# A mixture-of-experts layer in 10 slots of four 32-place parts instead of 12 slots of two 64-place halves, with the next attention's keys split five and three

## What is computed

```python
def _L0_ffn_ref(hidden_states, router_w, gate_w, up_w, down_w):
    H, I, E = (256, 512, 8)
    x = hidden_states.reshape(-1, hidden_shape[-1])
    route = jax.nn.sigmoid(x @ router_w)
    max_ind = jnp.argmax(route, axis=1)
    max_prob = jnp.take_along_axis(route, max_ind[:, None], axis=1)
    for e in range(num_experts):
        mask = (max_ind == e)[:, None]
        h = jax.nn.silu(x @ gate_w[e]) * (x @ up_w[e])
        out = out + jnp.where(mask, h @ down_w[e], 0.0)
    out = out * max_prob

x = x + tanh(g_xattn[0]) * _L0_xattn_ref(_layernorm(x), ctx, ...)
x = x + tanh(g_ffn[0])   * _L0_ffn_ref(_layernorm(x), ...)
x = x + tanh(g_xattn[1]) * _L1_xattn_ref(_layernorm(x), ctx, ...)   # k = rms_norm(linear(ctx, k_w, k_b)), v = linear(ctx, v_w, v_b)
x = x + tanh(g_ffn[1])   * _L1_ffn_ref(_layernorm(x), ...)
```

## Time and profile before

| | us |
|---|---|
| median of 3 runs (740.77 to 741.91) | 741.28 |
| the profiled execution | 739.69 |
| its span, first to last instruction | 738.0 |
| PE busy in it, share | 715.3, 97% |
| ACT, DVE, POOL busy, share | 347.1 (47%), 429.1 (58%), 268.6 (36%) |
| keys and slot 0, from its first matmul to slot 1's | 100.56 to 111.09 |
| slots 1 and 2 | 111.09 to 121.21 |
| slots 3 to 10 | 121.21 to 170.14 |
| slot 11 and the last down part | 170.14 to 180.09 |

### The profile page before, as it was taken

How to read it: one execution, slowest core, us unless ns; L and a number is a source line. 1 busy time by engine, 2 the same in 40 slices (tenths; PEclk the granted TensorE clock), 3 DMA queues, 4 the chain that set the end, 5 groups by cost and what they waited for, 6 DMA issues and landing times.

```text
span 738.0 us, 13906 instructions
## 1 busy us (share of the span) xinstructions
PE 715.3 (97%) x4748; PEld 575.9 (78%) x4749; DVE 429.1 (58%) x796; ACT 347.1 (47%) x815; POOL 268.6 (36%) x387
## 2 busy tenths in 40 slices
PE   7999899999899999999999999999999999999997
PEld 6888654444677888899888999888788888888886
DVE  6888574222898755444554445545566665666565
ACT  4888323442677736455454454544532323232333
POOL 3232351111877656312213222121433444344330
PEclk9999999999999999999999999999999999999999
DMA  8980121111200001111010110100034343333421
GB/s 281 419 351 1 30 72 38 47 45 60 78 16 1 24 1 36 28 53 37 21 36 21 57 36 21 64 1 22 22 77 127 99 121 114 113 100 120 126 80 58
DMA packets 23497, 56.36 MB, mean 76 GB/s; under 512 B 3472, under 2 KB 12048, under 8 KB 22432
## 3 DMA queue, kind: packets, MB, share of 16 engines
q1 hardware_dynamic: 22688, 53.72, 22.1%
q0 software_dynamic: 768, 2.10, 0.9%
HBM read 50.49 MB, written 5.31 MB: 76 GB/s over the span
## 4 chain that ended last, share of the span: by engine, by line
PE 84%; ACT 5%; DVE 5%; POOL 3%; DMA 1%; issue 1%; SPq 0%; DVEq 0%; POOLq 0%; ACTq 0%
PE PS L352 17%; PE PS L354 17%; PE PS L353 16%; PE PS L1850 7%; PE PS L1516 6%; PE PS L1537 3%; PE PS L470 3%; PE PS L476 2%; PE PS L516 2%; PE PS L507 2%; PE PS L1856 2%; PE PS L529 2%; POOL Z L854 1%; ACT x_probT L683 1%; PE PS L458 1%
## 5 line engine op out<-in xcount | busy, mean ns | idle before, releaser
L1296 ACT ACTIVATE hhh<-hh 128x512 fp32r<-128x512 f32 x50 | 31.6, 632 | 103.7 <-DVE hh L1318 94.7
L352 PE MATMUL PS<-tTh,wh 128*128 128x512 f32 x200 | 78.3, 392 | 0.8 <-DVE tTl L673 0.5
L353 PE MATMUL PS<-tTl,wh 128*128 128x512 f32 x200 | 77.8, 389 | 0.0
L354 PE MATMUL PS<-tTh,wl 128*128 128x512 f32 x200 | 77.8, 389 | 0.0
L673 DVE TENSOR_TENSOR hhl<-hh,hhh 128x512 fp32r<-128x512 f32 x50 | 52.4, 1047 | 35.4 <-ACT hhh L1296 35.4
L1959 ACT ACTIVATE sm<-sm,nmx 128x128 f32<-128x128 f32 x128 | 49.7, 389 | 37.7 <-DVE nmx L2022 37.7
L1384 POOL CAST wh<-wraw 128x512 fp32r<-128x512 f32 (+1 forms) x50 | 26.1, 523 | 108.6 <-PE PS L354 108.6
L2061 POOL CAST ah<-araw 128x512 fp32r<-128x512 f32 (+1 forms) x32 | 16.2, 506 | 134.4 <-PE PS L354 134.4
L673 DVE TENSOR_TENSOR oTl<-PS,oTh 128x512 fp32r<-128x512 f32 x32 | 22.1, 691 | 71.6 <-ACT oTh L1953 71.6
L1386 POOL TENSOR_TENSOR wl<-wraw,wh 128x512 fp32r<-128x512 f32 (+1 forms) x50 | 58.0, 1161 | 8.4 <-POOL wh L1384 7.9
L352 PE MATMUL PS<-tTh,ah 128*128 128x512 f32 x128 | 53.1, 415 | 0.3 <-POOL al L2063 0.2
(11 more groups left out here) (279 smaller groups left out, 1903.2 us busy)
## 6 DMA issues: line engine op xcount, KB each, us to landing
WE<-moe SPq DMA_DIRECT2D x8, 1536.0 KB, 17.8
wraw<-moe SPq DMA_DIRECT2D x25, 384.0 KB, 3.1
araw<-attn SPq DMA_DIRECT2D x16, 384.0 KB, 3.1
cwb<-cw_d SPq DMA_DIRECT2D x20, 256.0 KB, 3.9
WX<-wx SPq DMA_DIRECT2D x4, 512.0 KB, 6.8
avraw<-attn_v SPq DMA_DIRECT2D x8, 256.0 KB, 3.2
cwb<-cw_d SPq DMA_DIRECT2D x4, 448.0 KB, 3.5
xs_d<-zeros SPq DMA_DIRECT2D x1, 1536.0 KB, 20.5
```

The source lines that it names most:

```text
L352: nc.tensor.matmul(out, wh_, xh_, start=first, stop=False, **kw)
L353: nc.tensor.matmul(out, wh_, xl_, start=False, stop=False, **kw)
L354: return nc.tensor.matmul(out, wl_, xh_, start=False, stop=last, **kw)
L1296: nc.scalar.activation(hhh[half][:, :], hh[half][:, :], ACT.Copy).then_inc(s.hi_done, 1)
```

## The change

`HALVES` of 64 places become `TILES` of 32: 1024 / 32 + 8 = 40 parts, four to a slot (`PARTS`), and 10 slots. The loop over slots turns twice instead of three times. Each round of matmuls of a slot now has four strips of 32 columns: part 0 reads `WE` at the register's address, parts 1 to 3 read fixed places, `part_weights`. Gate's stand in `WX[0]` (the first attention's weights, no longer used) and `w2`, up's in `w2`, down's in `w2` and in `FX` (the scattered rows, rows 0 to 3), and for the last slot in the gate's places. `y_s` moves into rows 4 and 5 of `FX`.

So nine copies of 128x1024 are made for a slot where there were three. ACT makes up's three, triggered by the end of up (`u_done`) instead of standing behind the x columns. DVE makes two of gate's, triggered by the end of gate (`g_done`), ahead of hs. POOL makes gate's third at `g_done`, and down's three for slot j when down of j-1 is done (before: one for j+1 when down of j was done). Slot 0 and the last slot have lists of their own. PE waits for all copies of a part ahead of its first matmul.

Of the keys, five batches instead of six are made ahead of and in slot 0 (`SOON` = 5), three behind the last. The filling matmuls ahead of the last transposes of keys go from 14 to 8, and ACT's masked keys of batch 1 move behind `queries(1)` in the attention's loop.

```diff
-HP = P // 2
-HALVES = T // HP + E0
-SLOTS = HALVES // 2
+PARTS = 4
+HP = P // PARTS
+TILES = T // HP + E0
+SLOTS = TILES // PARTS
+GU = C * I0
...
+SOON = 5
...
-        below = sb("below", [P, HALVES, E0], where=e)
+        below = sb("below", [P, TILES, E0], where=e)
...
-        exf = sb("exf", [P, HALVES], where=e)
-        ex = sb("ex", [P, HALVES], mybir.dt.int32, e)
+        exf = sb("exf", [P, TILES], where=e)
+        ex = sb("ex", [P, TILES], mybir.dt.int32, e)
...
-        w2 = sb("w2", [P, EW], where=e)
+        w2 = sb("w2", [P, 6 * GU], where=e)
+        part_weights = [[WX[0][:, q, :, :].rearrange("p c n -> p (c n)") for q in range(2)] + [w2[:, 0:GU]],
+                        [w2[:, k * GU:(k + 1) * GU] for k in (1, 4, 5)],
+                        [w2[:, k * GU:(k + 1) * GU] for k in (2, 3)] + [FX[:, 0:I0 // P, :].rearrange("p k n -> p (k n)")]]
...
-        y_s = [sb(f"y_s{i}", [P, D], where=e) for i in range(2)]
+        y_s = [FX[:, I0 // P + i, :] for i in range(2)]
...
-                for b in range(2):
+                def masked_keys(b):
...
+                masked_keys(0)
...
-                key_columns(act, MOST, B)
+                key_columns(act, SOON, B)
             def value_rows_back(n):
...
+                if n == -1:
+                    masked_keys(1)
...
-        def half_expert(eng, j, h):
-            return eng.value_load(ex[0:1, bass.ds(2 * j + h, 1)], min_val=0, max_val=E0 - 1)
+        def part_expert(eng, j, q):
+            return eng.value_load(ex[0:1, bass.ds(PARTS * j + q, 1)], min_val=0, max_val=E0 - 1)
...
+        def down_weights(j):
...
+            return part_weights[0 if is_last(j) else 2]
...
+        def part_copy(eng, e, mat, q, done, j=0):
+            dst, src = (down_weights(j) if mat == 2 else part_weights[mat])[q - 1], expert_part(e, mat * GU, GU)
+            if eng is nc.scalar:
+                m = eng.activation(dst, src, ACT.Copy)
+            else:
+                m = eng.tensor_copy(dst, src)
+            m.then_inc(done, 1)
...
         def expert_part(e, a0, n):
...
             def up(e, j, par, mat, done):
...
+                if mat == 0:
+                    pe.wait_ge(s.gate_copied, 2 * j + 2)
+                    pe.wait_ge(s.gate3_copied, j + 1)
+                else:
+                    pe.wait_ge(s.up_copied, 3 * j + 3)
...
-                    a0 = (mat * C + c) * I0
-                    out, x = PS[:, 2 * mat + par, :], xsT[par][:, c, :]
-                    nc.tensor.matmul(out[0:HP, :], x[:, 0:HP], expert_part(e, a0, I0), start=(c == 0), stop=(c == C - 1))
-                    pe.wait_ge((s.gate_copied, s.up_copied)[mat], 2 * j + c + 1)
-                    m = nc.tensor.matmul(out[HP:P, :], x[:, HP:P], w2[:, a0:a0 + I0], start=(c == 0), stop=(c == C - 1))
+                    for q in range(PARTS):
+                        w = expert_part(e, (mat * C + c) * I0, I0) if q == 0 else part_weights[mat][q - 1][:, c * I0:(c + 1) * I0]
+                        m = nc.tensor.matmul(PS[q * HP:(q + 1) * HP, 2 * mat + par, :], xsT[par][:, c, q * HP:(q + 1) * HP], w, start=(c == 0), stop=(c == C - 1))
...
             def turn_hidden(j):
...
             def down(j, par, between=None):
-                e = half_expert(pe, j, 0)
+                e = part_expert(pe, j, 0)
...
-                    a0 = 2 * C * I0 + k * D
-                    out = PS[:, 6 + par, 0:D]
-                    nc.tensor.matmul(out[0:HP, :], src[:, k, 0:HP], expert_part(e, a0, D), start=(k == 0), stop=(k == I0 // P - 1))
...
-                        pe.wait_ge(s.down_copied, j + 1)
-                    m = nc.tensor.matmul(out[HP:P, :], src[:, k, HP:P], w2[:, a0:a0 + D], start=(k == 0), stop=(k == I0 // P - 1))
+                        pe.wait_ge(s.down_copied, 3 * j + 3)
+                    for q in range(PARTS):
+                        w = expert_part(e, 2 * GU + k * D, D) if q == 0 else down_weights(j)[q - 1][:, k * D:(k + 1) * D]
+                        m = nc.tensor.matmul(PS[q * HP:(q + 1) * HP, 6 + par, 0:D], src[:, k, q * HP:(q + 1) * HP], w, start=(k == 0), stop=(k == I0 // P - 1))
...
             def tile(j, par, i):
-                e = half_expert(pe, j, 0)
+                e = part_expert(pe, j, 0)
...
-                    keys_values(5)
...
-                    pe.wait_ge(s.kv_free, 2 * MOST)
+                    pe.wait_ge(s.kv_free, 2 * SOON)
...
-            for i in range(MOST, B):
+            for i in range(SOON, B):
+                if i == B - 1:
...
+                    pe.wait_ge(s.y_ready, SLOTS - 1)
...
-                if i == MOST:
+                if i == SOON:
...
-                    fill(14, 2)
-                pe.wait_ge(s.k1_ready, 1 if i < MOST else 2)
+                    fill(8, 2)
+                pe.wait_ge(s.k1_ready, 1 if i < SOON else 2)
...
             def tile(j, par, i):
-                e = None if is_last(j) else half_expert(act, j + 1, 1)
+                es = [] if is_last(j) else [part_expert(act, j + 1, q) for q in range(1, PARTS)]
...
-                    gate_copies(e)
...
-                    return
-                if not is_second(j):
-                    hidden_columns(j - 1)
+                else:
+                    if not is_second(j):
+                        hidden_columns(j - 1)
+                    if not is_last(j):
+                        columns(j + 1, 1 - par)
...
-                    columns(j + 1, 1 - par)
-                    gate_copies(e)
...
-            def gate_copies(e):
-                for c in range(C):
-                    nc.scalar.activation(w2[:, c * I0:(c + 1) * I0], expert_part(e, c * I0, I0), ACT.Copy).then_inc(s.gate_copied, 1)
+                    act.wait_ge(s.u_done, j + 1)
+                    for q, e in enumerate(es):
+                        part_copy(nc.scalar, e, 1, q + 1, s.up_copied)
...
-            gate_copies(half_expert(act, 0, 1))
+            es = [part_expert(act, 0, q) for q in (3, 2)]
+            part_copy(nc.scalar, es[0], 0, 3, s.gate3_copied)
...
+            part_copy(nc.scalar, es[0], 1, 3, s.up_copied)
+            part_copy(nc.scalar, es[1], 1, 2, s.up_copied)
...
-            key_columns(act, 0, MOST)
+            key_columns(act, 0, SOON)
...
         def kv_bank(i):
...
-            return PS[:, (1, 7, 3)[i % 3] if i < MOST else 4 + i - MOST, :]
+            return PS[:, (1, 7, 3)[i % 3] if i < SOON else 4 + i - SOON, :]
...
         def normalise_keys(dve, i0, i1, group):
...
-            def up_copies(e):
-                for a0 in (C * I0, (C + 1) * I0):
-                    v.tensor_copy(w2[:, a0:a0 + I0], expert_part(e, a0, I0)).then_inc(s.up_copied, 1)
...
             def tile(j, par, i):
-                e = None if is_last(j) else half_expert(dve, j + 1, 1)
+                if not is_last(j):
+                    es = [part_expert(dve, j + 1, q) for q in (1, 2)]
+                    dve.wait_ge(s.g_done, j + 1)
+                    for q, e in enumerate(es):
+                        part_copy(v, e, 0, q + 1, s.gate_copied)
+                else:
+                    dve.wait_ge(s.g_done, j + 1)
...
+                    dve.wait_ge(s.down_copied, 3 * j)
+                    part_copy(v, part_expert(dve, j, 1), 2, 1, s.down_copied, j)
...
-                if not is_last(j):
-                    up_copies(e)
...
-                    keys_values(4, MOST)
+                    part_copy(v, part_expert(dve, 0, 1), 2, 1, s.down_copied)
+                    keys_values(4, SOON)
...
-                    normalise_keys(dve, 0, MOST, 1)
+                    normalise_keys(dve, 0, SOON, 1)
...
+            es = [part_expert(dve, 0, q) for q in (1, 2)]
...
-            up_copies(half_expert(dve, 0, 1))
+            for q, e in enumerate(es):
+                part_copy(v, e, 0, q + 1, s.gate_copied)
+            part_copy(v, es[0], 1, 1, s.up_copied)
...
-            keys_values(MOST, B)
+            keys_values(SOON, B)
...
         def gather(b):
...
-            def down_copies(e):
-                nc.gpsimd.tensor_copy(w2[:, 2 * C * I0:EW], expert_part(e, 2 * C * I0, EW - 2 * C * I0)).then_inc(s.down_copied, 1)
...
             def tile(j, par, i):
...
-                    keys_power(0, MOST, 1)
+                    keys_power(0, SOON, 1)
...
-                    e = half_expert(pool, j + 1, 1)
-                    pool_wait(pool, s.d_done, j + 1)
-                    down_copies(e)
+                    e = part_expert(pool, j + 1, 3)
+                    pool_wait(pool, s.g_done, j + 1)
+                    part_copy(nc.gpsimd, e, 0, 3, s.gate3_copied)
+                if is_last(j):
+                    es = [part_expert(pool, j, q) for q in (2, 3)]
+                    pool.wait_ge(s.g_done, j + 1)
+                    for q, e in enumerate(es):
+                        part_copy(nc.gpsimd, e, 2, q + 2, s.down_copied, j)
+                elif not is_first(j):
+                    es = [part_expert(pool, j, q) for q in range(1, PARTS)]
```

(7 more changed lines are left out.)

16 lines of the change are left out of this document (8 added, 8 removed).

## The result

The changed kernel takes **733.02 us** (median of 4 runs, 731.37 to 733.72) against 741.6 for the kernel before in the same series (4 runs, 740.77 to 743.08): ratio 0.9879, 95% interval 0.9856 to 0.9902. Forecast was 733.4 with a range of 731.8 to 738.3. The profiled execution of the changed kernel took 732.96, its span is 731.3 (738.0 before).

The account below looks back on a forecast made before the run. TensorE, busy for 97% of the span, was taken to bound the kernel. The terms -12.2 + 3.3 + 0 + 1.0 = -7.9 us took the median of 741.28 to 733.4 us, range 731.8 to 738.3.

Parts of the forecast that it names:

- Slots (-12.2): Loop over slots: four-strip rounds cost the same as two-strip ones, so two slots of 6.12 us go, -12.2 us.
- Rival (3): All rounds of all ten slots: four strips don't stream at full rate; 746 us at a quarter longer rounds; chance 0.08.
- Copies in the steady slots (0): Steady slots: nine weight copies a slot on ACT, DVE and POOL fit within the 6.12 us period, 0 us.
- The margins: Steady slots: POOL's third down copy was to end 0.25 us before its part is due, the gate copies 0.3 us.
- First slots (+3.3): Start of the slots: added routing work and copies delay slot 2's up part from 117.72 to 121.0, +3.3 us.
- Last slot (0): Last slot: early down copies save 0.85 to 1.4 us, later hs costs 0.9 to 1.9; together 0.
- the delay of hs: Last slot: DVE's down copy, with its waits and load, stands ahead of hs and delays it by 0.9 to 1.9 us.
- Keys (+1.0): One key batch moved from the first slot to behind the last: x_xn of row 0 later, +1.0 us (0.7 to 1.7).
- Taking it out of the front gives nothing: First slot: the moved key batch lay in waits there, so removing it gains 0 us.
- x_xn of row 0: Second attention: this row was to come some 7.9 us earlier than 188.90, as a sign in the changed profile.

Follow-up runs that it names:

- e1_keys6: Changed kernel with six batches of keys at the first slot instead of five, two behind the last, 14 filling matmuls: 731.89 us, ratio 0.9883 to the kernel before.
- after: First profile of the changed kernel itself, against the kernel before: median 733.02 us, ratio 0.9879; the profiled execution took 732.96 us.
- e0_after: The changed kernel run again with no edit, beside its variants on the same chip: 733.11 us, ratio 0.9892 to the kernel before.
- e2_slots12: Changed kernel with 48 places of parts instead of 40, hence 12 slots, the last two without tokens: 748.21 us, ratio 1.0101 to the kernel before.
- e9_orders_keys: Changed kernel with hs first, POOL's and ACT's slot 0 work reordered, loop written out, six key batches, no added filling matmuls: 732.98 us, ratio 0.9892 to before.

## Why the prediction was right, point by point

**Slots (-12.2): right.** Six slots take 36.97 to 37.07 us with one jump back and 36.63 without; a slot of four strips is 6.10 to 6.13. Rival (3) is out: rounds are 0.43 and 0.21 with four strips. The factor of 2.38 for three strips, which the Trainium skill gives (TensorE: Matmul & The Clock Gate, "Measured speedup vs the span model"), is not seen with these fp32 matmuls, since four strips here cost no more than two.

**Copies in the steady slots (0): right, but for a pause that I did not have.** No copy holds TensorE in the slots from 3 to 9: POOL's third down copy of the rows above ends at 129.78, ahead of the down part at 130.50, its gate copy at 131.23, ahead of 132.23. The margins are 0.7 and 1.0 where I had 0.25 and 0.3. DVE and POOL take turns: two DVE copies, 1.31 alone (at 101.14), take 2.14, and POOL's take 1.50 for 1.04, the wait for DVE's being inside the record. This fits whole instructions in turn: 1.50 is 1.04 and 0.46 of waiting. The Trainium skill (SBUF — State Buffer, "Who interferes with whom") says that one blocks the other for the whole instruction; the trace agrees, and adds that DVE's second copy doesn't go ahead of a POOL copy that waits. ACT's three copies take 2.95 (1.08 each assumed), and end 0.39 to 0.58 before its Silu is due. What I had not was the jump back of the loop: +0.3 to +0.4, shown by two kernels.

**First slots (+3.3): right at equal clock.** From the routing's start to slot 2's up part 34.13 us at full clock, 30.83 before: **+3.30**. In parts: the routing and the first copies +0.65 (14.32 for 13.67), the two slots +2.65. The 34.13 is of a kernel with filling matmuls; without them the four profiles with full clock at the routing (14.31 to 14.36) and the two of the changed kernel with full clock in the slots (19.80, 19.82) give the same 34.1 to 34.2. The changed kernel as it is needs 36.30, since it runs for about 7 us at half clock, which costs 2.1 to 2.2 (16.38 to 16.48 for 14.3). Comparing only the two first profiles I would have read +5.5 and called the term wrong.

**Last slot (0): wrong by 1.0, in the good sense.** It took 8.95 for 9.96. The step that failed is the delay of hs, put at 0.9 to 1.9. DVE's wait for POOL's copies (3.58 us) lay in time in which DVE had nothing else, and the load was covered by that wait, so hs began 4.87 us behind the last gate part (163.16) instead of 4.38, 0.5 later; against it POOL's 0.85 and the drain of the rounds before went in full.

**Keys (+1.0): right behind the last slot** (9.83 for 8.81, and 1.17 back when undone). "Taking it out of the front gives nothing" was wrong: it gives 1.35 there, since the sixth batch stands ahead of POOL's power and slot 1's gate part (POOL's 1.66 us wait in `e1_keys6`). I had compared with the kernel before, in which that chain had slack, and not with the changed one, in which it holds TensorE. The whole edit is worth about 0, not +1.0, though the sum is right: the gain in front was already inside the +3.3, which was worked out with five batches.

**Sum.** At equal clock -12.2 + 0.4 (jump) + 0.15 (slot 2) + 3.3 - 1.0 + 1.0 = -8.4; with 2.2 of the half clock -6.2; the earlier start of the routing in the changed profile (0.73) and a longer rest (0.26) make the 6.7 by which the spans differ. By medians it is 7.9 to 8.6, more than the 6.7 of the spans, since the profile of the kernel before lies 1.6 to 1.9 us below its medians (739.69; 741.28, 741.6). The forecast of -7.9 thus held with two terms off that cancel in part: the last slot better by 1.0, and the clock, not foreseen, worse by up to 2.2 (the kernel before has a clock under 1.000 too, in most of its runs). The terms at equal clock (-8.4) are what the prediction got right; that the medians come within 0.7 us of -7.9, with the half clock on both sides, is partly luck. One sign of the prediction was missed, too: x_xn of row 0 came at 181.94, 6.96 us earlier than before instead of 7.9.

**What stays open.** Where the half clock comes from. Twelve profiles of kernels with ten slots stand in the table: in six it began at the routing, in four in slot 0, in one a short one came in each, and in one, with slot 0's waits filled, in neither. In slot 0 it came in or behind a wait of TensorE of 1.9 to 2.4 us each time; but three of the six profiles that had it at the routing (`after`, `e0_after`, `e1_keys6`) have such a wait in slot 0 too (1.92 to 1.93), and kept 1.00 there. From 84 to 88 TensorE is busy for 3.4 us in all profiles without a filling matmul there, before included, and for 3.6 to 3.8 in the others. That the filling matmuls hold the clock isn't shown: two other kernels had them and fell at the routing, and the three are the same on TensorE up to slot 0; of their runs three of four, none of four (the one of 2482 us aside) and one of five were at 1.000. The Trainium skill (TensorE: Matmul & The Clock Gate, "HAM oscillation — how this bites in real kernels") puts such falls down to waits of TensorE; slot 0 agrees where it fell there, the three that kept 1.00 and the routing aren't explained by it. The kernel before with such filling matmuls wasn't run, so how much of the gain by medians is due to the clock on either side is not settled: its runs, too, show 0.994 to 1.000.

## What to carry to other kernels

Where a bounding engine works in slots of a fixed price, fewer and fuller slots pay their full price, and what is given back lies at the two ends, where the covers of the steady state are missing: walk through each engine's list there, instruction by instruction, and ask of every moved step what it waits for and who waits for its result (a sixth batch put behind two copies held the power of the keys, and through it a gate part by 2.1 us). Compare the clock of stretches before comparing the stretches: 2 us of 5.5 in the start were half clock in unchanged code, and so was one experiment's whole gain of 1.2.

## What the runs showed of the hardware that was not expected

- Stretches at half clock of 3 to 10 us, at the routing or in slot 0, in a kernel whose TensorE is busy for 96% of the span. They cost 2.1 us in the one place and up to 3.5 in the other (23.27 for 19.80). With nine filling matmuls in the waits three of four runs had 1.000, and the kernel took 2.75 us less; kernels with the same filling matmuls up to slot 0 fell all the same.
- TensorE's jump back in a loop of two slots with four strips costs 0.3 to 0.4 us each time; with two strips, half as many instructions, the slots of the earlier trace rows and those behind them show none (6.11 to 6.12 throughout).
- DVE and POOL, both copying 128x1024, alternate by whole instructions, 1.27 and 1.25 us on average (from 126.1 to 163.16) instead of 0.65 and 1.04. A mean square of DVE (128x256) beside a copy of POOL's took 1.86 and 1.29 us instead of 0.41, in two of the fourteen profiles (`e2_slots12`, `e9_orders_keys`), and moved hs by 1.4 us in the first.
